# Who issues the writes of a unit's parts: GpSimd behind its own subtraction, or the sync engine

## The reference, cut to what matters

```
qkv = layernorm(x) @ Wqkv                       # q, k, v per head, (8, 16, 1024, 16)
num = exp(einsum(q_rot, k_rot) * scale)
den = sum(exp(einsum(q, k) * scale), axis=-1)   # over all 1024 keys
attn = where(causal, num / den, 0)
x = x + (attn @ v) @ Wout + bout
x = x + ffn(layernorm(x))                       # squared-relu, shared expert and routed ones
```

## Time and profile before

| | |
|---|---|
| median of three runs | 1865.06 us (1864.2 to 1865.12) |
| profiled execution | 1872.72 us, its span 1871.0 us |
| ACT busy | 1601.1 us |
| PE busy | 1549.3 us |
| DVE busy | 825.2 us |
| POOL busy | 505.0 us, 868 instructions |
| mean granted clock of TensorE | 0.941 |
| DMA | 172.40 MB, all of the program's own issued by SP |

### The profile page before, as it was taken

One profiled execution on the slowest core, in us unless ns is written; L12 is line 12 of the kernel. 1 busy time (PEld: TensorE's weight loads), 2 busy tenths in 40 slices (PEclk: granted clock), 3 DMA queues, 4 the chain that ended last, 5 costly groups with the idle time before them and its releaser, 6 DMA issues.

```text
span 1871.0 us, 29149 instructions
## 1 busy us (share of the span) xinstructions
PE 1549.3 (83%) x8362; PEld 619.2 (33%) x8416; DVE 825.2 (44%) x1824; ACT 1601.1 (86%) x2633; POOL 505.0 (27%) x868
## 2 busy tenths in 40 slices
PE   3578988789788897888977887988978889778995
PEld 1222323233333333233332333323432333323333
DVE  4223433374334653355533644347423565235415
ACT  0589997899798997899978998989978999789990
POOL 3123232232232321333222313223123422124210
PEclk8799998999899998999989999999989999899986
DMA  4345433443544424454234545345254451444400
GB/s 117 77 102 116 93 88 67 94 110 72 125 101 90 111 53 102 100 124 102 63 88 97 121 86 117 84 94 115 61 108 102 103 120 39 99 102 94 102 23 23
DMA packets 88878, 172.40 MB, mean 92 GB/s; under 512 B 9344, under 2 KB 75904, under 8 KB 76416
## 3 DMA queue, kind: packets, MB, share of 16 engines
q1 hardware_dynamic: 88704, 170.31, 40.9%
HBM read 111.55 MB, written 58.72 MB: 91 GB/s over the span
## 4 chain that ended last, share of the span: by engine, by line
issue 32%; PE 26%; ACT 20%; POOL 9%; DVE 5%; DMA 5%; SPq 1%; DVEq 0%; ACTq 0%; POOLq 0%
ACT scores L463 13%; PE scores L505 7%; ACT probs L473 6%; PE y_ps L534 5%; PE scores L512 4%; POOL parts L386 4%; PE side L564 3%; DMA qk_parts<-parts 3%; POOL rot L384 2%; DMA stack<-qk_parts 2%; PE side L585 1%; POOL x_acc L414 1%; PE side L544 1%; SPq L313 1%; PE side L571 1%
## 5 line engine op out<-in xcount | busy, mean ns | idle before, releaser
L463 ACT ACTIVATE scores<-scores 128x1024 f32<-128x1024 f32 x1024 | 1046.6, 1028 | 23.9 <-PE scores L505 22.7
L473 ACT ACTIVATE probs<-scores 128x1024 f32<-128x1024 f32 x512 | 491.3, 1025 | 188.6 <-PE scores L512 186.7
L505 PE MATMUL scores<-stack 96*128 96x512 bf16 x2048 | 581.8, 385 | 59.2 <-ACT probs L473 25.5
L512 PE MATMUL scores<-stack 96*128 96x512 bf16 (+3 forms) x1536 | 345.2, 340 | 142.2 <-DMA stack<-qk_parts 123.1
L534 PE MATMUL y_ps<-probs,v_sb 128*32 128x512 f32 (+3 forms) x3072 | 331.3, 503 | 5.9 <-ACT probs L473 4.8
L376 POOL TENSOR_SCALAR_AFFINE_SELECT probs<-probs 128x256 f32<-128x256 f32 (+1 forms) x640 | 223.5, 375 | 372.6 <-ACT probs L473 218.5
L505 PEld LDWEIGHTS scores<-stack 96*128 96x128 bf16 x2048 | 161.2, 98 | 426.9 <-ACT scores L463 200.4
L512 PEld LDWEIGHTS scores<-stack 96*128 96x128 bf16 x1536 | 126.8, 100 | 420.6 <-issue 183.0
L384 POOL TENSOR_TENSOR rot<-raw,cos_sb 128x512 f32<-128x512 f32 x64 | 89.9, 1405 | 584.1 <-DVEq L831 584.1
L386 POOL TENSOR_TENSOR parts<-rest,parts 128x512 bf16<-128x512 f32 x128 | 147.7, 1154 | 343.5 <-DVE parts L818 337.2
L463 ACT ACTIVATION_READ_ACCUMULATOR scores<-scores 128x1 f32 x1024 | 205.5, 201 | 0.0
(11 more groups left out here) (110 smaller groups left out, 1123.6 us busy)
## 6 DMA issues: line engine op xcount, KB each, us to landing
qk_parts<-parts SPq DMA_DIRECT2D x128, 384.0 KB, 2.6
stack<-qk_parts SPq DMA_DIRECT2D x128, 384.0 KB, 6.3
stack<-qk_parts SPq DMA_DIRECT2D x128, 256.0 KB, 6.8
stack<-qk_parts SPq DMA_DIRECT2D x128, 128.0 KB, 7.6
x_in<-in_L_attn_x SPq DMA_DIRECT2D x8, 1024.0 KB, 5.4
out<-x_mid SPq DMA_DIRECT2D x32, 256.0 KB, 6.9
probs<-in_L_attn_Wqkv SPq DMA_DIRECT2D x1, 512.0 KB, 6.6
cos_sb<-in_cos SPq DMA_DIRECT2D x1, 512.0 KB, 7.3
```

The lines of the kernel that those rows point to most:

```text
L463: nc.scalar.activation(src, src, ACT.Exp, scale=SCALE, accum_out=den[:, g % 2, i, j:j + 1]).then_inc(exp_done, 1)
L473: nc.scalar.activation(probs[:, chunk % 2, j, :], src, ACT.Exp, scale=SCALE).then_inc(exp_done, 1)
L505: mm = nc.tensor.matmul(tile[:, half * HALF:(half + 1) * HALF], q[:, j, i * P:(i + 1) * P], k[:, j, half * HALF:(half + 1) * HALF], start= ...
L512: mm = nc.tensor.matmul(tile[:, col:col + n], k[:, h, i * P:(i + 1) * P], q[:, h, q0:q0 + n], start=True, stop=True)
```

## The change

The write of a part leaves SP's queue and is issued by POOL, right behind the subtraction that completes the part. Before the first write of a unit POOL waits for `stacked` of the unit before, which SP did till now; before each write it waits for its own subtraction's `low_ready`. SP keeps the fills, with their wait for `plain_sent` or `rot_sent`, and the wait for the scores of the unit that used the buffer. In unit 3 the output writes of two block pairs, which stood behind the writes of each half, now stand behind the fills of each kind.

```diff
-                if not (isinstance(b, int) and b == 0 and g == 0):
-                    sp.wait_ge(stacked[1 - parity], at(b, 2 * 12 * 16, (g + parity) // 2 * 12 * 16))
-                    sp.sem_inc(held["sp"], 1)
-                for half in range(2):
-                    for kind, sent in ((0, plain_sent), (1, rot_sent)):
-                        sp.wait_ge(low_ready, at(b, 16, 4 * g + 2 * half + kind + 1))
+                for kind, sent in ((0, plain_sent), (1, rot_sent)):
+                    if kind == 0 and not (isinstance(b, int) and b == 0 and g < 2):
+                        sp.wait_ge(scores_ready, at(b, G * NSTEP, (g - 1) * NSTEP))
                         sp.sem_inc(held["sp"], 1)
-                        sp.dma_start(scratch[kind, :, :, :, half * HALF:(half + 1) * HALF].rearrange("c s r t -> (s r) c t"),
-                                     parts[:, kind, :, :]).then_inc(sent, 16)
-                        if half == 1:
-                            if kind == 0 and not (isinstance(b, int) and b == 0 and g < 2):
-
-                                sp.wait_ge(scores_ready, at(b, G * NSTEP, (g - 1) * NSTEP))
-                                sp.sem_inc(held["sp"], 1)
-                            fill_stacks(b, g, kind, sent)
+                    fill_stacks(b, g, kind, sent)
                     if outs is not None:
-                        send_out(outs, half)
+                        send_out(outs, kind)
...
                 nc.gpsimd.tensor_tensor(parts[:, t % 2, 2, :], rest[:, :], parts[:, t % 2, 1, :], ALU.subtract
                                         ).then_inc(low_ready, 1)
+                if t == 0 and not (isinstance(b, int) and b == 0 and g == 0):
+                    parity = g % 2
+                    pool.wait_ge(stacked[1 - parity], at(b, 2 * 12 * 16, (g + parity) // 2 * 12 * 16))
+                    pool.sem_inc(held["pool"], 1)
+                half, kind = t // 2, t % 2
+                pool.wait_ge(low_ready, at(b, 16, 4 * g + t + 1))
+                pool.sem_inc(held["pool"], 1)
+                pool.dma_start(scratch[kind, :, :, :, half * HALF:(half + 1) * HALF].rearrange("c s r t -> (s r) c t"),
+                               parts[:, kind, :, :]).then_inc((plain_sent, rot_sent)[kind], 16)
```

## The result

The changed kernel takes 1879.62 us in the median of nine runs (1875.4 to 1885.7), the kernel before 1865.12 us on the same chip. The ratio is 1.0081, with a 95% interval of 1.0066 to 1.0097: 0.8% slower, where 1829 us had been forecast. The profiled execution took 1884.6 us.

The account below looks back on a forecast made before the run. It took PE's waits for operand-tile fills at units 0 and 1 as the bound: 49 us less 22.4 (16x) gives 26.6, plus 9.6 for the clock, 36.2 us, so 1829 us in the median, range 1803 to 1870.

Parts of the forecast that it names:

- What bounds the kernel: PE's waits for operand-tile fills at the starts of units 0 and 1: 123.1 us, time lost to the span.
- It leaves on its own queue about when it is ready, beside the plain fills: Rotated half-1 write on POOL's queue: rot fills get queued before the plain fills end, so the DMA engines don't pause.
- rival A: Write on POOL's queue lands no sooner, engines being full with fills: 6 us gained, 1859; chance 0.16 together with C.
- the 49 us: Gain over the stalls before subtracting 16x: 7 x 3.4 for units 0, 9 x 2.8 for units 1 and the start.
- 21.4: Us from first plain fill to last landing after the change, both fill sets and the write behind one lead and tail.
- x: Plain half-1 write's extra time from subtraction's end to landing, over SP's 0.1 + 2.6 us; forecast 1.4, break-even 3.1.
- The Trainium skill's 0.4: Alternative x from first-byte times, about 1 us on the GpSimd path against 0.6 on SP's; sum then 42.6 us.
- Rival B: POOL hands transfers over late, so slower: 1888 by its own work (chance 0.12), 1878 by DVE's lock (0.10).
- What the POOL time hides behind: About 180 us more POOL time, covered by the product's 1.6 us lead, masks and the fill stall: cost 0.
- the masks: POOL's masks behind the writes: PE waits 0.7 us more in unit 3, swallowed by the fill stall; unit 0 covers 1.7.
- The clock: TensorE's clock halves in unit 1's stalls; shorter stalls save 2.4 us in half of eight: 9.6 us.
- a stall of 2.6 us just escapes the fall: Unit 1's stall, 4.0 - 1.4 us after the change, stays under the 2.8 us idle time at which TensorE's clock falls.

Follow-up runs that it names:

- e4: Kernel before, all writes on SP, rotated half-1 write after three of six plain fills, output writes behind fills: 1809.8 us against 1860.0, ratio 0.9724; expected 1820 to 1840.
- e1: Kernel before with only the rotated half-1 write (t = 3) issued by POOL: 1858.0 us against 1860.0, ratio 0.9991.
- e5: Kernel before with the rotated half-1 write on ScalarE's hardware queue, the very first unit's left on SP: 1856.3 us against 1860.6, ratio 0.9971.
- e6: Changed kernel with the last three plain fills held until POOL issued the rotated half-1 write, output writes behind all fills: 1846.2 us; 1860.6 before, ratio 0.9910.
- e3: Kernel before, all writes on SP; POOL waits for each subtraction, then runs two memsets (about 0.7 us), sending nothing: 1863.7 us against 1860.0, ratio 1.0017.
- e7: Kernel before with only the rotated half-0 write (t = 1), for which no fill waits, on POOL: 1867.2 us against 1860.6, ratio 1.0025.
- e2: Kernel before with writes t = 0, 1, 2 on POOL, the rotated half-1 write on SP, output write in its old place: 1880.3 us against 1860.0, ratio 1.0105.
- e8: Kernel before with only the plain half-1 write (t = 2), for which the plain fills wait, on POOL: 1882.8 us against 1860.6, ratio 1.0110.

## Why the prediction was wrong, point by point

**What bounds the kernel: right.** The fills at the starts of units 0 and 1 are the place; without the pause 50 us go (e4).

**"It leaves on its own queue about when it is ready, beside the plain fills": here it failed.** The write left 0.57 us after its subtraction, but landed 9.35 us later at the median (8.3 in the profile of before, on SP's queue): 9.9 us behind its subtraction, where the prediction had called itself wrong over 5.7. The step took a landing of 2.6 us from writes that had idle engines in front of them and gave it to one with up to 1.5 MB of fills in front. That was rival A, and all of the 49 us hung on it. e1 and e5 show the same 8.6 us from two queues, e4 and e6 show that the place among the fills decides. So the rot fills went behind a pause as before, 23.9 us from the first fill to the last landing in unit 0 and not 21.4. Only unit 3, where the write came early enough in some batches, got 1.0 us on average. The Trainium skill (DMA: Bandwidth & Descriptors, Queues, rings and completion order) says that an engine round-robins between the queues that have work, packet by packet; by that the write would have come through beside the fills. In unit 0 of the changed kernel it didn't (no packet of its queue from 549 to 554 us). In e6, where the write and three fills come together, the halves of 50.3% and 47.3% agree with it; what the write can't do is share with fills that were issued before it. Why, is not shown. The same page of the Trainium skill, in its section Issuing engines are not separate DMA queues, says that another issuing engine saves only the time of issue. That sentence agrees with e1 and e5, and it should have been a rival of its own.

**Rival A's price was summed wrongly.** It came out at 1859. It let x work on the rotated write alone and let this write land 8.3 us after an earlier issue. Its landings were right: 9.7 us behind the subtraction for the fills that move in unit 3 and 10.1 for those in unit 0 were forecast, 9.7 and 9.6 measured. But it left out that the plain fills start x later too, so that in unit 0 the end comes x later, however early the rotated write leaves. With x = 0.95 in each of the 16 stalls and no gain, A gives 1865 + 15 = 1880, near the measured 1879.6, and this is in part luck: POOL's time (4 us, below) is missing in it, and so is unit 3, whose first fill came 0.4 us earlier instead of 0.95 later and whose fills took 1.0 us less.

**The size of x: nearly right.** Forecast 1.4, measured 0.57 + 3.05 = 3.62 us from subtraction to landing against 2.67, so 0.95. The Trainium skill's 0.4 (DMA: Bandwidth & Descriptors, Specifications) falls short here, since half of the difference is POOL's wait for its own subtraction and the landing itself takes 0.5 us longer (3.05 against 2.57 us). Rival B's long descriptor work didn't come: 0.80 us an issue. Nor did the issues get longer by DVE: the 128 took 784 to 944 ns. But for the rule of the Trainium skill (SBUF — State Buffer, Who interferes with whom) that is a weak test, since a cast ran beside only 9 of them, and began 0.3 to 0.4 us into the issue (those 9 took 784 to 789 ns). In the other direction there is a sign. Such a cast, of 0.43 us alone, begins 0.45 us ahead of the rotation product, during POOL's issue, and still ends behind the product:

```profile
536.22 0.79 POOL L385 DMA_DIRECT2D qk_parts<-parts  x1 [0.57 <-POOL parts L376]
537.02 1.29 POOL L374 TENSOR_TENSOR rot<-raw,cos_sb 128x512 f32<-128x512 f32 x1
...
536.57 2.03 DVE L811 CAST parts<-raw 128x512 bf16<-128x512 f32 x1
```

Whether it is the issue that holds the cast up to the product, no run separates.

**"What the POOL time hides behind": wrong for t = 1.** I took the 1.6 us idle time ahead of the t = 2 subtraction for cover of the rotation product. It was no slack, for POOL's product holds up DVE's cast, and the subtraction waits for what DVE does next. Before, DVE's cast starts with the product and ends just behind it; after, it ends just behind it as well, so a later product makes everything behind it later. The cover is the 0.92 us that POOL waits for DVE's copy ahead of the product (e3); a hold of 1.37 costs 0.5 us in unit 0, some 4 us in all. e7, with this hold alone, measured 6.6 us (2 to 7). For the masks I was right in kind: PE waited for them 13.1 us in 15 places, against once, 1.1 us, before.

**The clock: not tested by the change**, whose stalls of unit 1 stayed (3.9 us on average, 4.1 before). e4 shows what it is worth. Here are 5 us about the start of unit 1 in the batch that I follow, before and in e4 (the last column but two is the granted clock):

```profile
564.00:569.00 5.00, 5.00 (x9) 1.84 (x8) 0.00 (x0) 2.05 (x2) 0.00 (x0) 0.50 0.00 0
...
541.00:546.00 5.00, 4.41 (x23) 1.73 (x22) 1.67 (x3) 5.00 (x9) 0.29 (x1) 1.00 0.00 0
```

So it is in all eight units 1: at the lower level at their start before, at the upper one in e4. From the first activation to the sixth it takes 6.5 to 8.0 us before and 4.6 to 5.4 in e4, 2.5 us less on average, near the forecast's 2.4, and in all eight units instead of half: 20 us, more than the 10 by which e4 beats its expectation. A part comes back, for in three of the eight the clock falls 5 to 6 us later (0.50 from 550 to 555 us), and unit 1 as a whole is 1.6 us shorter. And that a stall of 2.6 us just escapes the fall doesn't hold: in e6 the clock is at the lower level at the start of unit 1 behind four stalls of 1.6 to 1.9 us, and not behind three of 1.2 to 1.5.

**The sum as measured:** 16 x 0.95 = 15 and 8 x 0.5 = 4 us make 19, against 14.5 in the changed kernel (12 to 18 by its interval) and 20.3 in e2 (16 to 23). The two intervals overlap, and the two profiled executions took the same, 1884.6 and 1884.7 us, so the 6 us between them need no cause. What the changed kernel has less than the sum would fit unit 3, where the fills took 1.0 us less; e2, with this write on SP, has 23.8 us there. The single prices of e7 and e8 (6.6 and 22) add to more than e2's 20.3. To some 7 us the account stays open.

## What to carry to other kernels

A transfer that has to overtake others must be issued ahead of them; another engine's queue doesn't let it pass what was issued before. So look for the place in the one order, here in the middle of the fills that don't need it, where enough work stands behind it to cover its own landing. And before a wait of an engine is called cover, ask whether what it waits for would move along with the work that is pushed into it. Here the wait ahead of the product was cover, and the longer one behind it was not.

## What the runs showed of the hardware

A write of 384 KB lands 2.6 us after its issue from SP and 3.05 us from POOL when nothing is in front, and 8.6 us from POOL or from ACT (e1, e5), 9.35 in the changed kernel, with the plain fills in front. POOL's issue of it takes 0.80 us. Packets of POOL's queue are larger: 14336 for 50.3 MB, while SP's made the difference of 51,200 (88704 - 37504) for the same bytes, and the busy share for these is 8.3% against 9.7% (40.9 - 31.2). A DMA from POOL that waits for POOL's own last instruction starts 0.57 us behind its end; SP's starts 0.10 us behind it. A write on another queue moves behind the fills that were issued before it, and shared the engines half and half with those that came with it (e6, 541 to 543 us). The largest surprise is the size of the pause: 1.2 us of engine work in a write, and 3.4 us between first fill and last landing hung on where it stood.
